# Splitting the opening of a two-layer adaLN kernel: two batches ahead of the first projection, six between the first two attentions

## The reference, cut to what matters

```python
mod = (_silu(L0_c) @ L0_wmod).reshape(8, 6, 1, -1)     # 8 batches x 6 vectors of 128
sa, ca, ga, sb, cb, gb = mod[:, 0], ..., mod[:, 5]
ga = (2 * (ga >= 0) - 1) * jnp.maximum(jnp.abs(ga), 0.25)   # gb alike
h = _layernorm(x) * (1 + ca) + sa
x = x + ga * _L0_attn_ref(h, Wq, Wk, Wv, Wo, rel_bias)
h = _layernorm(x) * (1 + cb) + sb
x = x + gb * _L0_ffn_ref(h, w_q, w_k, w_gate, value_experts, output_experts)
# layer 1: the same with L1_c, L1_wmod and the weights of layer 1
```

## Time and profile before

| what | us |
|---|---|
| median of 3 runs (lowest, highest) | 807.25 (806.21, 807.82) |
| the profiled execution, its own time | 807.88 |
| its span in the trace | 805.8 |
| first score of batch 0 on DVE | 34.5 |
| `values(0)` begins on PE | 56.8 |
| PE busy, share of the span | 94% |

### The profile page before, as it was taken

The page is one execution under the profiler, slowest core; times in us unless marked ns, Lnnn a source line. Parts: engine busy times, 40 slices in busy tenths (PEclk is TensorE's granted clock), DMA queues, the critical chain, the costliest instruction groups (busy, mean ns, idle before and its releaser), DMA issues.

```text
span 805.8 us, 16963 instructions
## 1 busy us (share of the span) xinstructions
PE 760.5 (94%) x6585; PEld 577.1 (72%) x6585; DVE 547.0 (68%) x1639; ACT 404.5 (50%) x1105; POOL 182.4 (23%) x232
## 2 busy tenths in 40 slices
PE   3889999999999999999999999999999878999994
PEld 2765765874877588658766876687587757999984
DVE  5548837769666876677677868677859453255695
ACT  1665535355535654564456435623651466554563
POOL 1132113062115301530252034204302231000000
PEclk9999999999999999999999999999999998999998
DMA  8922002302040204020311212030204340000000
GB/s 238 343 70 53 1 2 54 89 18 54 2 106 1 54 2 106 2 53 24 84 27 28 59 49 53 2 87 20 54 2 106 106 106 1 1 1 2 8 21 26
DMA packets 53989, 42.57 MB, mean 53 GB/s; under 512 B 37852, under 2 KB 46700, under 8 KB 52504
## 3 DMA queue, kind: packets, MB, share of 16 engines
q1 hardware_dynamic: 53912, 41.51, 19.4%
HBM read 31.93 MB, written 9.58 MB: 52 GB/s over the span
## 4 chain that ended last, share of the span: by engine, by line
PE 85%; DVE 5%; ACT 4%; issue 2%; DMA 2%; POOL 1%; SPq 0%; ACTq 0%; DVEq 0%
PE ps L1491 13%; PE ps L1567 12%; PE ps L1599 7%; PE ps L1705 6%; PE ps L1693 6%; PE ps L1586 4%; PE ps L1654 4%; PE ps L1669 4%; PE ps L1477 4%; PE ps L1499 3%; PE ps L1521 3%; PE ps L1510 2%; PE ps L1450 2%; PE ps L1617 2%; PE ps L1426 2%
## 5 line engine op out<-in xcount | busy, mean ns | idle before, releaser
L1491 PE MATMUL ps<-veF,hB 128*128 128x512 f32 x256 | 121.4, 606 | 0.0
L1108 DVE COPY_PREDICATED shared<-ghot,ps 128x512 f32<-128x512 int32 x128 | 88.0, 725 | 3.3 <-PE ps L1491 0.6
L715 ACT ACTIVATE sc<-sc,nmax 128x128 f32<-128x128 f32 (+1 forms) x128 | 57.2, 447 | 59.4 <-DVE nmax L1094 59.4
L1491 PEld LDWEIGHTS ps<-veF,hB 128*128 128x128 f32 x256 | 45.3, 189 | 49.9 <-issue 40.2
L535 POOL TENSOR_TENSOR sc<-sc,rg 128x384 f32<-128x384 f32 x64 | 51.6, 827 | 69.8 <-DVE rg L1081 69.8
L1693 PE MATMUL ps<-hE,veF 128*128 128x256 f32 x256 | 59.5, 384 | 4.7 <-ACT early_masks L810 2.3
L1567 PE MATMUL ps<-early_masks,oeF 128*128 128x256 f32 x256 | 62.9, 385 | 0.5 <-issue 0.5
L527 POOL TENSOR_TENSOR sc<-sc,rdenA 128x512 f32<-128x512 f32 x32 | 32.5, 1040 | 133.5 <-DVE rdenA L1035 133.5
L1567 PE MATMUL ps<-wide,oeF 128*128 128x256 f32 x256 | 62.3, 386 | 0.0
L1599 PE MATMUL ps<-hC,early 128*64 128x128 f32 x1024 | 60.3, 275 | 1.6 <-ACT hC L636 1.6
L1599 PEld LDWEIGHTS ps<-hC,early 128*64 128x64 f32 x1024 | 55.5, 137 | 6.2 <-issue 4.3
(11 more groups left out here) (233 smaller groups left out, 1559.0 us busy)
## 6 DMA issues: line engine op xcount, KB each, us to landing
chosen<-hot_scratch SPq DMA_DIRECT2D x16, 512.0 KB, 5.8
v_scratch<-shared SPq DMA_DIRECT2D x16, 512.0 KB, 5.1
vg<-v_scratch SPq DMA_DIRECT2D x16, 512.0 KB, 5.5
veF<-in_L_ffn_value_experts SPq DMA_DIRECT2D x1, 2048.0 KB, 10.2
oeF<-in_L_ffn_output_experts SPq DMA_DIRECT2D x1, 2048.0 KB, 14.6
early<-in_L_attn_w_qkv SPq DMA_DIRECT2D x1, 1536.0 KB, 17.8
shared<-bias_scratch SPq DMA_DIRECT2D x2, 512.0 KB, 6.8
veF<-in_L_ffn_W SPq DMA_DIRECT2D x1, 1024.0 KB, 5.3
```

The costliest lines, as they stand in the source:

```text
L715: act.activation(v, v, ACT.Exp, bias=nmax[:, h % RING, t:t + 1], scale=-1.0, accum_out=denB[:, h * T + t:h * T + t + 1]).then_inc(s_("f_e" ...
L1108: dve.copy_predicated(val[:, t, :].rearrange("p (h k) -> p h k", h=HF), ghot[:, t * HF:(t + 1) * HF, e].bitcast(I32).unsqueeze(2) .broadca ...
L1491: pe.matmul(ps[:, vbank(j), :], tok(hB, t), veF[:, :].rearrange("p (h e k) -> p e h k", h=HF, e=EF)[:, e, :, :], start=True, stop=True).th ...
```

## The change

Only what the first two batches need stands ahead of the first projection; the rest of the opening is laid between the first two attentions, in new steps STATS, MOD1, NORMED and TURNED_ALL.

- Loads: `x` of batches 0 and 1 (0.25 MB), `wm0`, `wq`, `wk` come first; `wv` goes ahead of the reads of the bias table; the other 0.75 MB of `x` and `wm1` follow `wo`.
- Ahead of the first projection remain four statistics, a root of four variances, four normalisations, four transposes, the modulations of layer 0 (12 instructions instead of 24), and the folding of `wq` and `wk`. `wq` is now folded by PE (16 instructions) instead of by sums on DVE. `wv` is folded behind the projections of q and k, `wo` behind that of v; the reversed bias follows on ACT behind v.
- STATS (behind QK of batch 1, ahead of N0 of batch 0): the statistics of the other 12 tiles on DVE, and their root on POOL.
- MOD1 (behind T0 of batch 0, ahead of V0): modulations of layer 1 and `g8`, on PE and DVE.
- NORMED (behind S1 of batch 1, ahead of N0 of batch 1): 12 normalisations on DVE. TURNED_ALL (behind N1 of batch 1): 12 transposes on PE, the modulated input of batches 2 and 3 on ACT, 4 to 7 on DVE.
- GATES and GATED go behind T1 of batch 1 and behind MODULATE of batch 0; `values(0)` now waits for `gate1`.
- In batches 0 and 1 POOL multiplies one head of each pair by the reciprocals, DVE the other.
- `keys_added` goes from DVE to ACT, in four pieces beside `products(0)`.

```diff
             attn0(1, 0, TAKE)
             attn0(1, 0, QK)
-            gates(0, 0, GATES)
+            opening(0, 0, STATS)
             for n in (N0, N1, T0):
                 attn0(0, 0, n)
-            gates(0, 0, GATED)
+            opening(0, 0, MOD1)
             for n in (V0, T1):
                 attn0(0, 0, n)
             attn0(1, 0, S0)
             attn0(0, 0, V1)
             attn0(0, 0, OUT)
             attn0(1, 0, S1)
+            opening(0, 0, NORMED)
             after_attn0(0, 0, PROJECT)
-            for n in (VP, N0, N1, T0):
+            for n in (VP, N0, N1):
                 attn0(1, 0, n)
+            opening(0, 0, TURNED_ALL)
+            attn0(1, 0, T0)
             after_attn0(0, 0, ADD)
             attn0(1, 0, V0)
             after_attn0(0, 0, NORM)
             attn0(1, 0, T1)
+            opening(0, 0, GATES)
             after_attn0(0, 0, MODULATE)
+            opening(0, 0, GATED)
             for n in (V1, OUT):
                 attn0(1, 0, n)
...
# POOL
+            def root(lo, hi, n):
+                pool.wait_ge(s_("n_agg"), hi)
+                pool.tensor_tensor(ve[:, lo:hi], mv[:, lo:hi, 1], eps[:, lo:hi], ALU.add).then_inc(s_("n_ve"), 1)
+                pool.wait_ge(s_("n_ve"), n)
+                pool.tensor_tensor(rstd[:, lo:hi], ve[:, lo:hi], half[:, lo:hi], ALU.pow).then_inc(s_("n_rstd"), 1)
+            root(0, AHEAD * T, 1)
+            def opening(b, k, n):
+                if n == STATS:
+                    root(AHEAD * T, TILES, 2)
...
-                    for h in (2 * p, 2 * p + 1):
+                    for h in (2 * p, 2 * p + 1)[:1 if early_batch(b) else 2]:
...
# ACT
+            fold(0)
+            act.wait_ge(s_("mod_ready"), 1)
+            act.sem_inc(s_("n_h"), B)
+            first_input(0)
+            fold(1)
+            first_input(1)
+            fold(2)
...
+                if n == QKV and b == 0:
+                    bias()
+                    fold(3)
...
# DVE
+            def opening(b, k, n):
+                if n == STATS:
+                    loaded(dve, "x")
+                    first_stats(AHEAD * T, TILES)
+                if n == MOD1:
+                    link(modulations(1))
+                    ...
+                if n == NORMED:
+                    first_norm(AHEAD * T, TILES, 2)
+                if n == TURNED_ALL:
+                    for b in range(B // 2, B):
+                        ...
+                        dve.tensor_scalar(hE[:, b * N:(b + 1) * N], ps[:, first_bank(b), ...], ...)
...
+                    if early_batch(b):           # in N0 and N1, behind the reciprocal
+                        h = 2 * p + 1
+                        dve.wait_ge(s_("a_r"), b * 2 + p + 1)
+                        for t in range(T):
+                            v = sc[:, h, t * N:(t + 1) * N]
+                            dve.tensor_scalar(v, v, rdenA[:, h * T + t:h * T + t + 1], None,
+                                              ALU.mult).then_inc(s_("a_pd"), 1)
...
# PE
+            loaded(pe, "wm0")
+            modulations(0)
+            fold(0)
+            turn_first(0, AHEAD * T)
+            fold(1)
+            def opening(b, k, n):
+                if n == MOD1:
+                    loaded(pe, "wm1")
+                    pe.wait_ge(s_("w_ready"), 4)
+                    pe.matmul(ps[0:B, 0, 0:D], csT[:, 1, :], wm[1][:, 5 * D:6 * D], ...).then_inc(s_("g8_p"), 1)
+                    modulations(1)
...
             def values(b, k, beside):
                 beside("start")
                 normed(k)
+                if b == 0:
+                    pe.wait_ge(s_("gate1"), 2)
```

More of the change, by code:

```diff
@@ L44 @@
 TAKE, QKV, S0, S1, N0, N1, T0, T1, V0, V1, OUT = range(10, 21)
+STATS, NORMED, TURNED_ALL, MOD1, KEYS = range(30, 35)
 E1, F1 = 8, 256
@@ L221, in adaln_kernel @@
                   "tables": ["vadd", "same"], "tablesF": ["causal", "rankF"],
-                  "route": ["bits", "bitsf", "rm"], "experts": ["w1", "w2"], "mod": ["wm0", "wm1"],
-                  "bias": ["rb", "oneh"], "small": ["bsel"]}
+                  "route": ["bits", "bitsf", "rm"], "experts": ["w1", "w2"],
+                  "bias": ["rb", "oneh"], "small": ["bsel"], "first": ["x01"]}
         group_of = {n: g for g, names in groups.items() for n in names}
@@ L310, in vbank, with in_order @@
             return 1 + i % 3
-        def in_order(attn0, values, turns, front1, back1, products, masks, gates, last_softmax, after_attn0, after_products,
+        def in_order(attn0, values, turns, front1, back1, products, masks, opening, last_softmax, after_attn0, after_products,
                      after_front1, after_attn1):
@@ L381, in in_order @@
             values(0, 1, beside((after_attn0, 1, 1, in_values_first)))
-            products(0, beside((masks, 0, 0, first_masks), (attn0, 2, 0, in_products0)))
+            products(0, beside((masks, 0, 0, first_masks), (attn0, 2, 0, in_products0), (opening, 0, 0, keys)))
             round_(0, 2, first=True)
@@ L598, in after_attn1 @@
                     pool.tensor_copy(hE[:, bass.ds(b * N, N)], hR[:, :]).then_inc(s_("h_kept"), 1)
-            beside = in_order(attn0, values, nothing, front1, back1, products, nothing, nothing, last_softmax, after, after,
+            beside = in_order(attn0, values, nothing, front1, back1, products, nothing, opening, last_softmax, after, after,
                               after_front1, after_attn1)
@@ L836, in last_softmax @@
                 keep(0, 1)
-            beside = in_order(attn0, values, turns, front1, back1, products, nothing, gates, last_softmax, after_attn0,
+            beside = in_order(attn0, values, turns, front1, back1, products, nothing, opening, last_softmax, after_attn0,
                               after_products, after_front1, after_attn1)
@@ L1243, in after_attn1 @@
                                       lrec[:, :].unsqueeze(2).broadcast_to([P, T, E1]), ALU.mult).then_inc(s_("l_d"), 1)
-            beside = in_order(attn0, values, turns, front1, back1, products, masks, nothing, last_softmax, after_attn0,
+            beside = in_order(attn0, values, turns, front1, back1, products, masks, opening, last_softmax, after_attn0,
                               after_products, after_front1, after_attn1)
@@ L1335, in _, with fold @@
-            pe.matmul(ps[0:B, 7, 0:D], csT[:, 1, :], wm[1][:, 5 * D:6 * D], start=True,
-                      stop=True).then_inc(s_("g8_p"), 1)
-            for i in (2, 3, 0, 1):
+                mm.then_inc(s_("mod_p"), 1)
+            def fold(i):
                 loaded(pe, ("wq", "wk", "wv", "wo")[i])
-                if i < 2:
-                    pe.wait_ge(s_("w_sum"), i + 1)
+                if i == 1:
+                    pe.wait_ge(s_("w_sum"), 1)
+                if i == 2:
+                    pe.wait_ge(s_("bvec_done"), 1)
```

240 lines of the change are left out of this document (137 added, 103 removed).

## The result

The changed kernel takes 811.36 us in the median of five runs (810.51 to 812.41), against 807.01 for the kernel before on the same chip: a ratio of 1.0055 with a 95% interval of 1.004 to 1.007, so 4.35 us slower, where 812.8 was forecast. The profiled execution took 811.36 us with a span of 809.1, against 807.88 and 805.8 before. A second measurement on another chip gave 811.38 and a ratio of 1.006 (1.0043 to 1.0078), and up to the first value product its trace has the same marks to 0.03 us.

The account below looks back on a forecast made before the run. PE was taken as the bound (85% of the chain), so the start of values(0) counts one for one: +4.3 there and +1.3 for the clock on 807.88 gave 813.5, median 812.8; range 807 to 817.5.

Parts of the forecast that it names:

- To the first score: Opening up to the first score on DVE: at 25.1 us against 34.51, a gain of 9.4.
- Part 2: First score to V0 of batch 0: 14.6 us in series, V0 at 39.7 against 41.09; loses 8.
- the rival in which it holds: PE's clock stays high between 11 and 61 us: 5.7 back, no change; chance 0.1 faster, 0.12 within no change.
- the second stretch: PE at the lower clock again around values(0), after mostly waiting from 54 to 61 us: 1.3 us lost.
- Part 3: V0 to ADD of batch 0: first score of batch 1 at 44.4, reciprocal 50.8, ADD 55.9; loses 5.
- The pair: DVE's share of the split multiplications in batches 0 and 1: 1.45 us a pair, between 0.6 and 1.6.
- Part 4: ADD to values(0), which waits for ACT's gate1 copies: 61.1 us against 56.82, 4.3 later; loses 2.
- Nothing waits there long enough to give back a shift: From values(0) at 56.82 to 794.5 us PE is busy 721 of 738, so its shift counts one for one.
- The range: Whole kernel: 807 to 817.5 us, leaving out the fast end and a late opening together with a low clock.
- the terms that are named for it: Bounds of the split (-1.7, +0.3) and of a mark falling with or without the lower level (-3.4, +2).
- the rival in which the lower level holds longer: Opening: PE stays at the lower clock up to 28 us, first score at 31.7, total 817; chance 0.12.
- What costs nothing: keys_added on ACT, under 9 us beside products(0), and the later weight loads are free; one late piece under 1 us.

Follow-up runs that it names:

- PE kept busy: Changed kernel plus 56 dummy identity transposes on PE behind the projections of batch 1: 806.74 us, ratio 1.0007 to the kernel before.
- statistics and root: Changed kernel with STATS (DVE statistics and POOL's root) moved from ahead of N0 of batch 0 to behind N1: 802.25 us, ratio 0.995 to the kernel before.
- the root alone: Changed kernel with only POOL's root of 12 variances moved behind its two multiplications of batch 0: 809.68 us, ratio 1.0037 to the kernel before.
- the runs that were spared it: Changed kernel with the wait for gate1 moved inside values(0), run twice: 809.94 and 811.39 us, ratios 1.0056 and 1.0061 to the kernel before.

## Why the prediction was right, point by point

- **To the first score: 25.1 forecast, 24.40 measured.** The modulations began at 7.88 (8.3 taken); the first folds ran at the slow rate as taken (3.61 for 16, 3.5 taken), the later ones at the fast one (1.80). The running sum has a slip: 14.4, 1.3 and 1.2 make 16.9, not 16.6; the first projection began at 16.12.
- **Part 2, V0 at 39.7: 39.16.** The terms: statistics 3.3 against 3.14; root 2.6 against 2.56 (30.46 to 33.02); T0 1.75 against 1.97; the product for `g8` and MOD1 3.0 against 3.19, all at the clock expected, a granted 0.50. That T0 would run at half the clock was an estimate from the earlier trace rows, 0.52 in the kernel before, and no run shows the 1.75: the eight transposes took 1.97 in the changed kernel, at 0.50, and 1.09 with PE kept busy, at 1.00. The runs confirm the two steps ahead of T0: 5.57 for statistics and root, 2.57 for the root alone. Counted from the first score it is 14.76 against 14.6; that V0 came 0.54 early is the opening's doing.
- **The clock was under-sized.** I put it at 3.4 (T0, MOD1, V0) for the rival in which it holds; measured 4.26, because T1 and the first scores of batch 1 lie in the same stretch. That the upper level would bring the kernel back to no change was right, but by luck in part: the rival needed 5.7, with 1.3 at `values(0)` and 1.0 in the opening. With PE kept busy the second stretch was still there (3.14 for the first eight rows; granted clock 0.50 from 57.4 to 60.7) and the opening was not faster; 4.26 sufficed because the loss was 4.35 and not 5.6.
- **Part 3: 44.4, 50.8, 55.9 forecast; 44.32, 50.86, 55.91 measured.** The fit of the first is luck: from V0 to the first score of batch 1 it took 5.16 where 4.7 was to stay, since T1 (1.97) and the first scores ran at the lower level too, and V0's 0.54 made up for it. The pair was taken as 1.45 between bounds of 0.6 and 1.6; it took 1.50 beside POOL's multiplication and 0.63 beside POOL's root.
- **The earlier trace rows was misread.** The prediction has one instruction of L994 at 1.08 while POOL multiplied, and lets a pair cost from 0.6, two of 0.27 and the hand-over. But POOL multiplied from 37.53 to 41.56, and all three instructions of L994 that began in that time took long, 0.50, 1.08 and 1.08; the other 13, at 0.27, began when POOL was done:

```profile
37.53 4.04 POOL L527 TENSOR_TENSOR sc<-sc,rdenA 128x512 f32<-128x512 f32 x4 [3.77 <-DVE rdenA L1035]
39.15 1.50 DVE L994 TENSOR_SCALAR early<-oT,bqkvT 128x128 f32<-128x128 f32 x2
```

  So the row gave no ground for 0.6 beside a multiplication, and the choice near the held row was better founded than the prediction says. The same holds for a pair of the changed kernel: its first instruction takes 1.23 beside POOL's 1.04, and its second, 0.34, begins when POOL is done.
- **Part 4: `values(0)` at 61.1 forecast, 60.86 measured;** the second stretch at the lower level 1.3 against 1.44 (3.43 against 1.99 in the runs that were spared it). The shift behind it is 5.55 (the second half of L1582 at 64.68, against 59.13 before); 5.6 was the forecast.
- **"Nothing waits there long enough to give back a shift" failed by a microsecond.** That was the last step of the sum, on the earlier trace rows. The shift stands at 5.56 until 493 us and at 4.46 by the end (the last update of `x` on DVE begins at 806.59, against 802.13 before): 0.35 went near 550, where the kernel before had waited for POOL's root, 0.5 between 610 and 657, 0.2 near 672. The first two stand in the second trace of the changed kernel as well; the third does not, for there PE ran at the lower level (0.50) from 674.8 to 681.7 and not only from 678.2 to 681.6, and the shift at the end is 5.19. So 0.9 was given back by waits, and the rest varies with the clock from one execution to the next. The last store took 2.2 us instead of 3.35, which makes the spans differ by only 3.3, while the medians differ by 4.35; the longer store fits that one execution of the kernel before and not its others. What was given back is the larger part of the way from 812.8 to 811.36.
- **The range** of 807 to 817.5 does not come out of the terms that are named for it: -1.7 and -3.4 give 807.7, +0.3 and +2 give 815.1. Its upper end is that of the rival in which the lower level holds longer (817), whose 4 us are not derived from its first score at 31.7, 6.6 later than the forecast.
- **What costs nothing** held: the 12 transposes on PE appear on no step of the chain above, and the shift stays at 5.55 from `values(0)` past `products(0)`, where `keys_added` now lies on ACT.

## What to carry to other kernels

A step that is moved out of a wait does not vanish; it lands in a queue, and the question is who stands behind it there. Here DVE was idle for 11.5 us ahead of the first score and for 7.4 us ahead of MOD1, and the change put 3.3 us of statistics exactly between, in front of what PE waited for; moving one line by three steps was worth 1%. Price an idle stretch of PE by what it does to the clock of the work behind it: here the 7 us without work cost another 4.3.

## What the hardware showed that was not expected

- **Beside POOL's root DVE was not held; beside its multiplications it was, to their end.** With POOL's multiplications of batch 1 (1.04 each) the first instruction of DVE's pairs took 1232 and 1234 ns and ended 0.15 behind POOL's, though it had begun 0.05 ahead of it, as far as the profile's spans on POOL go; the second, begun behind POOL's, took 343 and 340. The second pair of batch 0 lay wholly inside POOL's root and took 0.62 for the two:

```profile
30.75 2.27 POOL L536 TENSOR_TENSOR rstd<-ve,half 128x12 f32<-128x12 f32 x1
31.23 0.62 DVE L1109 TENSOR_SCALAR sc<-sc,rdenA 128x256 f32<-128x256 f32 x2
```

  The 12 normalisations beside two multiplications lost 1.37 (4.54 against 3.17): one was held by each of the two (978 and 1076 ns against 335), and the other ten began when POOL was done.
- **A clock column of 1.00 is not always a measured clock,** and the change of level comes at different places in executions of the same work. The column also reads 1.00 where the trace has no record of the clock; the first record stands at 16.0 us in the changed kernel and at 19.8 with PE kept busy. Ahead of it only durations tell the level. With PE kept busy, the first projection, ahead of the added work, took

```profile
16.07 2.07 PE L1494 MATMUL ps<-hA,wqT 128*128 128x256 f32 x4 [0.69 <-POOL hA L556]
```

  where the changed kernel, from 16.12 on, took 1.13, and its first score came at 26.17 instead of 24.40. So a mark in the opening is known to a microsecond or two, not better, unless it is counted from the first score on.
